# Six windowed-attention layers in one kernel: a new order of work on five engines, both score masks from ScalarE, turned halves in two shared PSUM banks

## The reference

```python
def attn_layer(x, Wqkv, qs, ksc, Wo):          # x has been through shift_tokens
    q, k, v = split(x @ Wqkv, 3)               # 16 heads of 64, INNER = 1024
    q, k = l2norm(q) * qs, l2norm(k) * ksc
    q = q * cos * scale + rotate_half(q) * sin * scale
    k = k * cos / scale + rotate_half(k) * sin / scale
    # windows of 32 queries see 64 keys: their own window and the one before
    sim = einsum('bhwie,bhwje->bhwij', q, look(k)) * 8
    attn = softmax(where(mask, -max, sim), -1)
    return merge_heads(einsum('bhwij,bhwje->bhwie', attn, look(v))) @ Wo

def ffn_layer(x, g, bln, W1, b1, W2, b2):
    a, gate = split((layernorm(x) * g + bln) @ W1 + b1, 2)    # 341 each
    return a * gelu(gate, exact) @ W2 + b2

for i in range(6):
    x = attn_layer(shift_tokens(x), ...) + x
    x = ffn_layer(shift_tokens(x), ...) + x
```

## Time and profile before

| | |
|---|---|
| three runs, us | 4283.55, 4286.01, 4286.08 (median 4286.01) |
| span of the profiled execution, us | 4281.5 |
| TensorE busy | 4088.3 us (95%) |
| ScalarE busy | 3716.8 us (87%) |
| VectorE busy | 3495.0 us (82%) |
| GpSimd busy | 2399.2 us (56%) |
| TensorE's mean granted clock | 0.978 |

### The profile page before, as it was taken

One profiled execution on the slowest core, in us unless ns is written; L12 is line 12 of the kernel. 1 busy time (PEld: TensorE's weight loads), 2 busy tenths in 40 slices (PEclk: granted clock), 3 DMA queues, 4 the chain that ended last, 5 costly groups with the idle time before them and its releaser, 6 DMA issues. The chain is left out here.

```text
span 4281.5 us, 124222 instructions
## 1 busy us (share of the span) xinstructions
PE 4088.3 (95%) x43826; PEld 2939.1 (69%) x43826; DVE 3495.0 (82%) x8236; ACT 3716.8 (87%) x7186; POOL 2399.2 (56%) x2876
## 2 busy tenths in 40 slices
PE   4999999987999999999999999999999999999995
PEld 2566666654777777777777777777777777777774
DVE  4788888866888888888888888888888888888884
ACT  4899999966998989989999899998999989999895
POOL 4000000026667776777777777777777777767763
PEclk7999999988999999999999999999999999999997
DMA  6777777741111111111111111111111111111111
GB/s 180 229 230 228 235 226 237 224 142 35 44 42 42 47 36 44 42 42 47 37 43 43 42 47 37 41 45 42 47 37 43 43 42 47 37 43 42 42 47 52
DMA packets 249884, 347.65 MB, mean 81 GB/s; under 512 B 45120, under 2 KB 206508, under 8 KB 249260
## 3 DMA queue, kind: packets, MB, share of 16 engines
q1 hardware_dynamic: 249388, 341.00, 26.8%
HBM read 151.13 MB, written 82.85 MB: 55 GB/s over the span
## 5 line engine op out<-in xcount | busy, mean ns | idle before, releaser
L1468 PE MATMUL la_ps<-la_Wqkv,la_xsT 128*128 128x512 f32 x2304 | 1181.3, 608 | 5.5 <-DVE X L1173 5.5
L1173 DVE TENSOR_TENSOR X<-la_ps,la_tab 128x1024 f32<-128x1024 f32 x768 | 934.3, 1217 | 116.8 <-ACT la_sq L1317 107.7
L1120 POOL TENSOR_TENSOR la_rt<-la_rt,la_rn 128x1024 f32<-128x1024 f32 x384 | 722.4, 1902 | 27.5
L1103 POOL TENSOR_TENSOR la_rt<-X 128x512 f32<-128x512 f32 x384 | 494.7, 1288 | 319.1 <-PE la_ps L1483 243.3
L1505 PEld LDWEIGHTS la_ps<-la_kT,la_qB 128*64 128x64 f32 x12288 | 389.3, 138 | 230.2 <-issue 218.8
L1180 DVE TENSOR_REDUCE la_ssum<-la_sq 128x8 f32<-128x512 f32 x768 | 503.2, 676 | 0.0
L1104 POOL TENSOR_TENSOR la_rt<-X 128x512 f32<-128x512 f32 x384 | 497.3, 1295 | 0.0
L1317 ACT ACTIVATE la_sq<-la_ps 128x512 f32<-128x512 f32 x768 | 457.7, 596 | 15.5 <-PE la_ps L1468 5.4
L1468 PEld LDWEIGHTS la_ps<-la_Wqkv,la_xsT 128*128 128x128 f32 x2304 | 377.9, 191 | 132.9 <-issue 93.5
L526 POOL COPY at_vh<-V 128x64 f32 (+1 forms) x64 | 15.1, 236 | 784.3 <-PE at_ps L725 783.2
L1505 PE MATMUL la_ps<-la_kT,la_qB 128*64 128x64 f32 x12288 | 442.4, 225 | 0.2 <-ACT la_kT L1349 0.2
(11 more groups left out here) (207 smaller groups left out, 9544.0 us busy)
## 6 DMA issues: line engine op xcount, KB each, us to landing
at_band<-skew_scratch SPq DMA_DIRECT2D x64, 1536.0 KB, 7.3
la_vs<-la_v SPq DMA_DIRECT2D x192, 384.0 KB, 3.5
skew_scratch<-at_R SPq DMA_DIRECT2D x64, 1024.0 KB, 6.6
la_vs<-la_v SPq DMA_DIRECT2D x192, 128.0 KB, 3.4
la_Wqkv<-in_wqkv SPq DMA_DIRECT2D x28, 384.0 KB, 4.7
at_qh<-qt_scratch SPq DMA_DIRECT2D x64, 144.0 KB
at_kh<-kt_scratch SPq DMA_DIRECT2D x64, 144.0 KB
la_W<-in_L_ffn_W SPq DMA_DIRECT2D x24, 341.0 KB, 4.5
```

The costliest lines, as they stand in the source:

```text
L1103: e.tensor_tensor(dst[:, :, 0, :], c[:, :, 0, :], s[:, :, 1, :], ALU.add)
L1120: e.tensor_tensor(heads(rt, w), heads(rt, w), wide(rn[:, w * H:(w + 1) * H], D), ALU.mult)\
L1173: e.tensor_tensor(dst.rearrange("p f (h d) -> p f h d", d=D), ps[:, c % 2, :].rearrange("p (h d) -> p h d", d=D).unsqueeze(1).to_broadcast ...
L1468: e.matmul(ps[:, c % 2, :], xsT[:, m * P:(m + 1) * P], Wqkv[:, ds(layer(n) % 2, 1), c * 512:(c + 1) * 512], start=True, stop=True)\
```

## The change

Four things are done, all in `layers`.

1. The order of each engine's list is new, for TensorE, ScalarE, VectorE, GpSimd and SyncE. The projections now have lag 2 where three of them had lag 3, and q is turned at lag 3 in both halves. On TensorE the scores and values of a body stand side by side, and each kind of transposition is done in both halves at once.
2. Both masks are written by ScalarE; TensorE's masking matmul and its bf16 mask and identity are gone.
3. The halves of q, k, p and of the output use banks 4 and 5 alternately instead of one bank for q and k and one for p and output. TensorE's waits name all the earlier users of a bank.
4. `turn_x` transposes x where it lies; GpSimd's copy is gone. One load at the start is gone with it.

In addition the Gelu table set is loaded explicitly ahead of `gelu` 0, and `gelu` 2 is done one body later.

```diff
-        BANK_S, BANK_T, BANK_P, BANK_F, BANK_Y = 2, 4, 5, 6, 7
-        N_IN, SET = 8, 7
+        BANK_S, BANK_F, BANK_Y = 2, 6, 7
+        TURNED_Q, TURNED_K, TURNED_P, OUT = (4, 5), (5, 4), (5, 4), (5, 4)
+        N_IN, SET = 7, 7
...
-            e.dma_start(sq[:, 0, 0:P], a["c_ident"]).then_inc(s_in, 16)
...
-            e.wait_ge(s_in, 16 * N_IN)
-            e.tensor_copy(mask[:], mask32[:])
-            e.tensor_copy(identb[:], sq[:, 0, 0:P]).then_inc(s_mask, 1)
...
-            def x_copied(n, m):
-                e.wait_ge(x_ev.sem, x_ev.v(n // 2 - NT // 2))
-                e.wait_ge(xT_mm.sem, xT_mm.v(n - 2))
-                x = X[:, ds(slot(n % NT), 1), :].rearrange("p l d -> p (l d)")
-                e.tensor_tensor(xc[:, m % 2, :], x, unit[:].to_broadcast([P, E]), ALU.mult).then_inc(xc_ev.sem, 1)
...
             def squares(n, m, c):
+                if c == 0:
+                    e.wait_ge(cl_ev.sem, cl_ev.v(n - 1))
...
             def turn_x(n, m):
-                e.wait_ge(xc_ev.sem, xc_ev.v(n))
-                e.transpose(ps[:, BANK_Y, 0:P], xc[:, m % 2, :], ident[:])\
-                    .then_inc(xT_mm.sem, 1)
+                e.wait_ge(x_ev.sem, x_ev.v(n // 2 - NT // 2))
+                e.transpose(ps[:, BANK_Y, 0:P], X[:, slot(n % NT), :], ident[:]).then_inc(xT_mm.sem, 1)
...
-            def masked(n, m, h):
-
-                e.wait_ge(nm_ev.sem, nm_ev.v(n - 1, h + 1))
-                e.matmul(ps[:, BANK_S + h, :], identb[:], over(mask[:, min(m, 1), :], 4), start=True, stop=True)
...
-                if h == 0:
-                    e.wait_ge(mk_ev.sem, mk_ev.v(n))
+                e.wait_ge(mk_ev.sem, mk_ev.v(n, h + 1))
...
+                for n, m in t.back(3):
+                    e.wait_ge(o_ev.sem, o_ev.v(n - 2, 2))
+                    e.wait_ge(pt_ev.sem, pt_ev.v(n - 2, 2))
+                    e.wait_ge(Tk_ev.sem, Tk_ev.v(n - 1, 2))
+                    e.wait_ge(Tq_ev.sem, Tq_ev.v(n - 1, 1))
+                    turn_q(n, m, 0)
+                    e.wait_ge(o_ev.sem, o_ev.v(n - 2, 1))
+                    e.wait_ge(pt_ev.sem, pt_ev.v(n - 2, 1))
+                    e.wait_ge(Tk_ev.sem, Tk_ev.v(n - 1, 1))
+                    e.wait_ge(Tq_ev.sem, Tq_ev.v(n - 1, 2))
+                    turn_q(n, m, 1)
```

More of the change, by code:

```diff
@@ L36 @@
 LN_AND_EXP = "natural_log_exp_and_others"
+GELU = "gelu_and_others"
 TILES = DEPTH * NT
@@ L1157, in body @@
                     root(n, m)
+                for n, m in t.back(3):
+                    newton(n, m)
+                    scaled(n, m, 0)
+                    scaled(n, m, 1)
+                for n, m in t.back(2):
+                    added(n, m, 0)
+                for n, m in t.back(7):
+                    with_b2(n, m)
             straight(e, body, TILES, TB, DEEPEST)
@@ L1262, in body @@
                     summed(n, m, 0)
+                for n, m in t.back(1):
+                    turned(n, m, 3)
+                for n, m in t.back(3):
+                    summed(n, m, 1)
+                    over_sum(n, m, 0)
+                for n, m in t.back(1):
+                    squares(n, m, 2)
+                for n, m in t.back(5):
+                    if m % 2:
+                        gated(n, m, 0)
+                for n, m in t.back(3):
+                    over_sum(n, m, 1)
+                for n, m in t.back(4):
+                    with_x(n, m)
@@ new lines, in body @@
+                for n, m in t.back(3):
+                    normal(n, m, 0)
+                for n, m in t.back(1):
+                    squares(n, m, 3)
+                for n, m in t.back(3):
+                    normal(n, m, 1)
+                for n, m in t.back(1):
+                    clipped(n, m)
+                for n, m in t.back(5):
+                    if m % 2:
+                        gated(n, m, 1)
+                for n, m in t.back(0):
+                    turned(n, m, 0)
+                    squares(n, m, 0)
@@ L1289, in body @@
-                for n, m in t.back(2):
-                    turned(n, m, 2)
-                for n, m in t.back(4):
-                    over_sum(n, m, 1)
-                for n, m in t.back(5):
-                    mean_over(n, m)
-                for n, m in t.back(4):
-                    normal(n, m, 1)
+                    stats(n, m)
             straight(e, body, TILES, TB, DEEPEST)
@@ L1399, in body @@
-                for n, m in t.back(3):
-                    squared(n, m, 3)
+                for n, m in t.back(7):
+                    if m % 2:
+                        e.preload_act_table_set(LN_AND_EXP)
+                for n, m in t.back(3):
+                    guess(n, m)
+                for n, m in t.back(4):
+                    masked(n, m, 1)
+                for n, m in t.back(5):
+                    p_turned(n, m, 1)
+                for n, m in t.back(2):
+                    squared(n, m, 2)
@@ L1421, in body @@
                 for n, m in t.back(6):
                     if m % 2:
+                        e.preload_act_table_set(GELU)
                         gelu(n, m, 0)
+                for n, m in t.back(3):
+                    q_turned(n, m, 0)
+                    q_turned(n, m, 1)
                 for n, m in t.back(2):
-                    squared(n, m, 0)
-                for n, m in t.back(3):
                     v_out(n, m, 5)
-                    q_turned(n, m, 0)
                 for n, m in t.back(6):
@@ L1568, in body @@
             def body(t):
+                for n, m in t.back(2):
+                    qkv(n, m, 1)
                 for n, m in t.back(0):
@@ L1615, in body @@
                         hidden(n, m, 0)
-                for n, m in t.back(2):
-                    qkv(n, m, 0)
                 for n, m in t.back(5):
@@ L1622, in body @@
                     out_proj(n, m)
[L1623 to L1626 removed]
+                for n, m in t.back(2):
+                    qkv(n, m, 5)
                 for n, m in t.back(6):
```

213 lines of the change are left out of this document (91 added, 122 removed).

## The result

Four runs took 4098.45, 4098.77, 4099.98 and 4101.48 us, median 4099.38. Against the kernel before, on the same chips (median 4284.78), the ratio is 0.9568, interval [0.9557, 0.958]: a gain of 185 us. The forecast was 4153 in a range from 4120 to 4250.

A forecast was written before the change was run, and what follows sets the result against it. TensorE, with no gap, was taken to bound the kernel at 33.48 us a pair; mask 0.42, tile size 0.62 and idle time 0.35 sum to 1.39, giving 32.1 a pair, -133 us over 96 pairs, 4153 in a range 4120 to 4250.

The forecast's parts named there:

- the chance of 0.87: Whole kernel: the probability given to faster, against 0.03 for the same and 0.10 for slower.
- Only the mask counts: Rival, TensorE: values to scores costs a full tile-size change, old idle time moves elsewhere; -40, 4246; shared chance 0.17.
- The GELU load: Rival, ScalarE: a second table load adds 1.28 a pair; -65, 4221; within the shared 0.17 for smaller gains.
- ScalarE become the bound: Rival: ScalarE keeps the old 3.3 of waits, pair 34.6, +108, 4394; half way +40, 4326; chance 0.10.
- The mask, -0.42: TensorE: two bf16 mask matmuls of 0.21 leave each pair, and all of it counts.
- The changes of tile size, -0.62: TensorE, scores and values: 64-wide tiles entered (0.10) and left (0.21) once a tile, not twice; -0.62 a pair.
- Two banks and idle time, -0.35: TensorE, turned halves in two banks: of 0.55 idle in a pair 0.2 is left; bounds -0.55 and 0.
- Scores behind values, taken as nothing: TensorE, values 0 to scores 1: change costs 0, bounds 0 and 0.31 of a full exit and entry.
- Filling and draining "taken as unchanged": Both ends of the layers: the same seven bodies, so no change in time.
- The lower end: Whole kernel: no idle at all and a cheaper change into the scores, 31.75 a pair, 4120.
- x, SyncE, GpSimd: Turning x from its home worth 0; SyncE's new order costs 0; GpSimd's chain to scaled q covered by 1 us.
- ScalarE +1.04: ScalarE: two mask steps of 0.52 a pair, own work from 30.18 to 31.2, off the path.

## Why the prediction came out as it did

**What bounds it, and which way: right.** TensorE's list is the time before and after; the chance of 0.87 was on the right side, and none of the rivals happened. "Only the mask counts" needed a full change of tile size from values to scores: scores 1 start 0.93 behind values 0 (2512.12), no more than the values' own. The GELU load did not double; the table loads are two in a pair, at L1401 and L1430. Nor did ScalarE become the bound, for it waits for TensorE hardly at all now (22.2 us in 85 pairs, 0.26 each, where it was 2.7). ScalarE's groups, 1212 to 3906 us, as in the earlier trace rows:

```profile
L1350 ACT ACTIVATE la_ps<-la_mask 128x512 f32<-128x512 f32 x341 | 207.1, 607 | 0.0
...
L1367 ACT ACTIVATE la_oT<-la_ps 128x512 f32<-128x512 f32 x341 | 202.3, 593 | 0.0
...
L1334 ACT ACTIVATE la_qB<-la_ps 64x512 f32<-64x512 f32 x340 | 199.2, 586 | 4.1
...
L1430 ACT ACT_TABLE_LOAD x85 | 109.1, 1283 | 1.5
```

The idle times 80.8 and 127.6 are 0.0 and 4.1.

**The mask, -0.42: right** (0.22 a tile by the run with `mean_over` early). The Trainium skill's stream figure of 131 ns ("TensorE: Matmul & The Clock Gate", "Back-to-back issue gap") would have made this 25 us, as an estimate; 43 were measured, so the trace's 0.21 stands here.

**The changes of tile size, -0.62: right in size, one entry counted twice in the old pair.** One more split a tile costs 60 us, 0.31 a tile. But the prediction's sum counts one of the four entries of the old pair twice. The one behind the feed-forward output lies in the 1.44 that it took for that output. After, it is 1.43 from 2526.57 to 2528.00, and by starts its instructions are 0.11 apart but the last one is 0.20 ahead of the scores: 1.34 is the output's own and 0.09 the entry. The other three stand behind projections, where the waits of the weight loads count them. Groups of scores' loads, before and after (busy us, mean ns | idle):

```profile
L1505 PEld LDWEIGHTS la_ps<-la_kT,la_qB 128*64 128x64 f32 x10368 | 328.5, 138 | 194.0 <-issue 184.2
```

```profile
L1499 PEld LDWEIGHTS la_ps<-la_kT,la_qB 128*64 128x64 f32 x10943 | 347.7, 138 | 74.7 <-issue 64.4
```

64.4 / 85 is 0.76 a pair, one entry behind a projection; 184.2 / 81 is 2.27, three of them. So four entries became two, and the term holds. But the entry counted twice made the old sum 0.10 too long, and so the idle time 0.10 too short.

**Two banks and idle time, -0.35: the first step that failed.** The pair was 33.48 and the sum, with that entry counted once, 32.8, so the real idle time was some 0.65, and the prediction left 0.2 of it in the new order. All of it went: -0.65. I had kept the 0.2 because three cushions in my layout were under 0.5. The layout itself was right to 0.2 us and held. By the timelines of ScalarE, GpSimd and TensorE's weight loads, counted from `qkv1` at 2507.41:

```profile
2512.01 0.59 ACT L1362 ACTIVATE la_pB<-la_ps 64x512 f32<-64x512 f32 x1
...
2515.18 0.59 ACT L1367 ACTIVATE la_oT<-la_ps 128x512 f32<-128x512 f32 x1
...
2521.10 0.59 ACT L1335 ACTIVATE la_qB<-la_ps 64x512 f32<-64x512 f32 x1
```

```profile
2513.24 3.76 POOL L1111 TENSOR_TENSOR la_rt<-la_rt,la_rn 128x1024 f32<-128x1024 f32 x2
```

```profile
2515.82 1.00 PEld L1476 LDWEIGHTS la_ps<-ident,la_rt 128*128 128x128 f32 x8 [0.47 <-ACT la_oT L1367]
```

p's second half ends at 5.19 (forecast 5.2; values 1 start at 5.65), the output copy at 8.36 (8.2; turning q 8.61), q's second half at 14.28 (14.3; turning k 14.72), scaling q at 7.73 (7.6). The smallest of these cushions is 0.25 us, and no matmul waits. It is less than it looks: the weight load of turning q does wait for that copy, and starts 0.05 behind it and 0.20 ahead of its matmul; the load itself lasts 0.14. Still the order costs nothing. It holds because the engines repeat themselves that closely: `mean_over`, which has 0.11 to spare in one body of the pair, took 148 to 154 ns in each of the 171 tiles from 1200 to 3891 us. What it has no room for is another step, as the four runs that moved one show (+22 to +157).

**Scores behind values, taken as nothing: a little better.** Scores 1 take 0.94 where the earlier trace rows have 0.98, -0.08 in a pair, which lies outside the prediction's bounds of 0 to 0.31 more.

Together 0.42 + 0.62 + 0.65 + 0.08 = 1.77 of the 1.82 measured. Over 96 pairs the 0.44 by which the pair is shorter than forecast is 42 of the 54 us between forecast and result.

**Filling and draining "taken as unchanged": the second step that failed.** The prediction's reason was that there are the same seven bodies. The lower end is a span of 4281.5 - 166.1 = 4115.4, and it was 4096.9, 18.5 less: 6.8 between the first and the last turn of x (172.9 for 166.1), 13.6 from the drain, and 2.0 back for the later start. The other 2 of the 20.6 us come from the step from span to run, 2.5 where 4.5 was added. So this term is the largest part of what put the time outside the range; without it the time would still have been some 7 us below. The times from the last turn of x to the last feed-forward output, and from the last but one such output to the last, read from TensorE's timelines:

| kernel | drain, us | last pair, us |
|---|---|---|
| before | 110.8 | 28.2 |
| before, mask 1 by ScalarE | 113.8 | 30.4 |
| changed | 97.2 | 24.4 |
| changed, mask 1 back | 98.3 | 24.5 |
| changed, mask 1 back, `mean_over` early | 100.6 | 24.5 |
| changed, copy of x first | 97.3 | 24.5 |
| changed, old banks | 119.0 | 24.9 |

With the new order the last pair takes 24.4 to 24.9, with the old one 28.2 to 30.4, wherever the mask is written, so the shorter last pair, 3.8 of the 13.6, belongs to the order (with the old banks the pairs ahead of it are long, as in the rest of that kernel). Most of the 13.6 is work. The drain as a window, before and then after:

```profile
4135.50:4246.30 110.80, 91.36 (x1057) 68.96 (x1055) 68.89 (x150) 78.60 (x145) 46.18 (x54) 0.93 0.13 36
```

```profile
3964.63:4061.84 97.21, 81.70 (x1038) 64.50 (x1036) 60.97 (x141) 75.20 (x141) 44.52 (x55) 0.93 0.09 25
```

TensorE's busy time fell by 9.7 us and its idle time by 3.9. The bodies are the same in number and not in content. With the shorter lags of the projections (2, and 1 for `qkv0`, where they were 3 and 2), 32 of their instructions are left behind the last turn of x where there were 42, five projections of 0.86 less; five masks of 0.21 are gone too, and half of the changes of tile size. The five projections are done in the filling instead, and did not make it longer: from the first turn of x to the first feed-forward output it takes 81.1 where it took 87.2, at a granted clock of 1.00 where it was 0.90 (81.0 to 84.4 in the runs with the new order, but for late copy and old banks, and 86.2 in the one with the old order). Which waits fell away in either was not tried.

**x, SyncE, GpSimd: nothing in the results speaks against them.** The copy of x at the head of GpSimd's list costs 1.5 us, inside the uncertainty. SyncE's new order was not tried by itself, but no matmul waits in the pairs. **ScalarE +1.04: too high, without effect.** Mask steps last 607 ns and stand 0.5 to 0.6 apart, but ScalarE's busy time rose by 0.6 in a pair, from 30.18 to 30.8 of 31.66, and not to 31.2. The durations of its instructions add up to 1.5 more in a pair; more of them overlap, as fewer wait.

**What the prediction did not see** is that the parts don't add. The mask was priced as 0.42 of TensorE's work wherever it is done; by itself, in the old order and at the one place tried, giving it to ScalarE costs 81 us. The banks were priced at 0.35; without them the new order loses 906. And the mask back on TensorE costs 43 or 93 us, by one VectorE instruction's place.

## What to carry to other kernels

Where one engine is full, sum its list by starts and lay the others beside it: here that gave each of the times compared above to 0.2 us, and cushions of 0.25 and 0.11 us cost nothing. But price a part of a hand-made order only in that order: by itself it costs what the steps that it makes late are worth (here a mask of 43 us cost 93, and moving it alone lost 81). And where the drain is some per cent of the time (here 97 of 4097 us), give filling and draining a term of their own: count by the lags what work is left in them, and expect waits beside it.

## What the hardware showed that I had not expected

**VectorE and GpSimd can exclude each other.** A VectorE instruction of one element in each partition, 0.15 us, lasted 1.82 us beside a GpSimd product of 1.90, and the time was back when it was moved ahead. `mean_over` reads and writes SBUF alone; VectorE's products of a projection, with one operand in PSUM, ran 1.21 to 1.23 beside the same GpSimd instruction. In the kernel before it was `clipped`, also in SBUF alone, that was hit now and then: it lasted over 0.26 us in 10 of all 192 tiles, and each time it ended 0.04 us behind one of GpSimd's sums (`added`). Its durations in the layers (ns):

```profile
L1186 DVE TENSOR_SCALAR la_hs<-la_ssum x161: 167/182/1337, 1215.2 to 3893.6; 128x32 f32<-128x32 f32 x161
```

The Trainium skill, page "SBUF — State Buffer", section "🔬 SBUF: two separate sides", says that VectorE and GpSimd share a port pair as an exclusive lock, held for a whole instruction, and names VectorE operations with two SBUF inputs among those that need it. The runs agree: the end of `mean_over` is the end of the GpSimd instruction to 0.02 us. The changed kernel avoids this by 0.11 us in one body of each pair. The prediction had no term for it, and the changed kernel needed none, by that luck of placing.

**The clock.** In the window from 2500 us the kernel with the late copy of x had a mean granted clock of 0.94 with TensorE busy 442.19 of 500 us, while the one with the old banks had 1.00, which is 2.4 GHz throughout, with only 403.78. The first has one wait of 2.3 us in a tile, and behind most of these the clock falls to 1.2 GHz for a while; the second has three waits of 2.0, 1.4 and 0.7. So it was not the sum of the idle time that lowered the clock; whether it was the longest wait was not tried.
